# A graph layer with an eigenbasis on one core: another chain in each tridiagonal step, eight normalisation units a step, and VectorE statistics for eleven late batches

## The reference

```
h = relu(layernorm(x))                        # per batch and node, over 1024 features
Ln = D^-1/2 (D - A) D^-1/2                    # one 120x120 matrix, from adj
_, U = eigh(Ln)                               # its eigenvectors
agg = U h;  z = relu(agg @ W1 + b1) @ W2 + b2
f = softmax(theta(z) maxpool(phi(z)));  y = f maxpool(g(z))
w = batchnorm(wo(y)) + z
out = x + U w + w
```

## Time and profile before

| | us |
|---|---|
| median of 3 runs | 3356.74 (3353.61 to 3360.74) |
| the profiled execution | 3357.3 |
| its span, first to last instruction | 3355.5 |
| stage 1, to the last update of `QA` | 0 to 467.7 |
| stage 2, to GpSimd's first `fetch` | 467.7 to 669.4 |
| stage 3 | 669.4 to 3355.5 |

### The profile page before, as it was taken

The page is one execution under the profiler, slowest core; times in us unless marked ns, Lnnn a source line. Parts: engine busy times, 40 slices in busy tenths (PEclk is TensorE's granted clock), DMA queues, the critical chain, the costliest instruction groups (busy, mean ns, idle before and its releaser), DMA issues.

```text
span 3355.5 us, 65816 instructions
## 1 busy us (share of the span) xinstructions
PE 3177.8 (95%) x16040; PEld 2546.3 (76%) x16040; DVE 2290.7 (68%) x6009; ACT 2415.3 (72%) x4380; POOL 1950.8 (58%) x2073
## 2 busy tenths in 40 slices
PE   6888886699999999999999999999999999999997
PEld 5667776577777777777777777777777777777775
DVE  7877779766666666666666666666666666666664
ACT  6888998856666666667666667767666666767665
POOL 4333322146666666666666666666666666666665
PEclk9999999999999999999999999999999999999998
DMA  3333343312222222222222222222222222222222
GB/s 95 94 95 100 102 108 99 91 37 71 72 74 74 76 72 71 71 71 71 72 74 73 71 71 71 71 71 71 71 73 75 75 73 71 71 71 71 72 74 68
DMA packets 111575, 256.22 MB, mean 76 GB/s; under 512 B 47500, under 2 KB 49797, under 8 KB 111493
## 3 DMA queue, kind: packets, MB, share of 16 engines
q1 hardware_dynamic: 111493, 255.25, 27.8%
HBM read 190.69 MB, written 63.44 MB: 76 GB/s over the span
## 4 chain that ended last, share of the span: by engine, by line
PE 80%; DVE 10%; issue 3%; POOL 3%; ACT 3%; DVEq 0%; DMA 0%; POOLq 0%; ACTq 0%; SPq 0%
PE ps_M L793 8%; PE ps_M L795 8%; PE ps_M L794 8%; PE ps_S L870 7%; PE ps_E L793 7%; PE ps_O L793 7%; PE ps_E L794 7%; PE ps_O L795 7%; PE ps_O L794 7%; PE ps_E L795 7%; PE ps_M L854 3%; POOL sc L449 1%; DVE u L1024 1%; DVE rown L1022 1%; ACT junkx L536 1%
## 5 line engine op out<-in xcount | busy, mean ns | idle before, releaser
L502 POOL TENSOR_TENSOR p_lo<-p,p_hi 128x512 fp32r<-128x512 f32 x1024 | 1381.2, 1349 | 932.0 <-ACT p_hi L653 928.9
L648 ACT ACTIVATE p<-ps_E 128x512 f32<-128x512 f32 x1024 | 614.1, 600 | 331.8 <-PE ps_E L795 307.0
L1388 DVE TENSOR_REDUCE nmx<-ps_S 128x1 f32<-128x512 f32 x1024 | 658.6, 685 | 129.1 <-PE ps_S L870 126.3
L653 ACT ACTIVATE p_hi<-p 128x512 fp32r<-128x512 f32 x1024 | 647.5, 632 | 32.6
L793 PE MATMUL ps_E<-o_hi,Q_hi 123*128 123x512 f32 x1024 | 426.7, 417 | 0.0
L793 PE MATMUL ps_O<-p_hi,v_hi 128*121 128x512 f32 x1024 | 406.7, 397 | 3.9 <-POOL p_lo L502 3.8
L795 PE MATMUL ps_O<-p_lo,v_hi 128*121 128x512 f32 x1024 | 406.4, 397 | 0.0
L794 PE MATMUL ps_O<-p_hi,v_lo 128*121 128x512 f32 x1024 | 404.6, 395 | 0.0
L794 PE MATMUL ps_E<-o_hi,Q_lo 123*128 123x512 f32 x1024 | 404.5, 395 | 0.0
L795 PE MATMUL ps_E<-o_lo,Q_hi 123*128 123x512 f32 x1024 | 403.7, 394 | 0.0
L1368 DVE TENSOR_REDUCE gf<-ps_M 128x256 f32<-128x512 f32 x256 | 177.1, 692 | 261.8 <-PE ps_M L795 261.8
(11 more groups left out here) (363 smaller groups left out, 5939.8 us busy)
## 6 DMA issues: line engine op xcount, KB each, us to landing
rbc<-r_dram SPq DMA_DIRECT2D x128, 484.0 KB
xin<-in_x_dram SPq DMA_DIRECT2D x128, 480.0 KB, 4.2
xt<-in_x_dram SPq DMA_DIRECT2D x128, 480.0 KB, 4.9
out_dram<-y SPq DMA_DIRECT2D x128, 480.0 KB, 3.7
o_hi<-mrow SPq DMA_DIRECT2D x256, 2.0 KB
dcol<-y SPq DMA_DIRECT2D x128, 4.0 KB, 2.0
r_dram<-rcol SPq DMA_DIRECT2D x128, 4.0 KB, 1.4
W1s<-in_L_gnn_W_dram SPq DMA_DIRECT2D x1, 512.0 KB, 4.4
```

The lines of the kernel that those rows point to most:

```text
L502: pool.tensor_tensor(p_lo[:, c % 4, :], p[:, c % 4, :], p_hi[:, c % 4, :].bitcast(F32), ALU.subtract).then_inc(plo_sb, 1)
L648: act.activation(p[:, c % 4, :], ps_E[c % 2][:, :], ACT.Exp).then_inc(p_sb, 1)
L653: act.activation(p_hi[:, c % 4, :], p[:, c % 4, :], ACT.Copy).then_inc(phi_sb, 1)
L1388: dve.tensor_reduce(nmx[:, c:c + 1], ps_S[SBANK[c]][:, :], AX.X, ALU.max, negate=True).then_inc(max_sb, 1)
```

## The change

**The step.** The sign of the pivot moves from GpSimd to VectorE (`sign()`, four one-element instructions behind the update of `QA`, with two gates that hold factors -2 and -4). GpSimd keeps the power alone. VectorE applies root and sign in one instruction, the gated reciprocal goes straight into `cu`, the two one-element products L1013 and L1015 go, and the next `u` is formed from `cu`, a part row and one scalar (`PAIR`) that no longer reads `zs`. `QA` has two halves that are written in turn.

**The rate.** 8 units a step in place of 9, the last 3 of them behind the update: 920 units are placed at the end of stage 1.

**Statistics on VectorE.** For eleven batches (85, 88, ..., 115) ScalarE does neither mean nor squares. SyncE loads them into a part of `P1` not in use yet (two buffers `xdv`), VectorE forms mean and variance with two `BN_STATS` of 512 columns, a `BN_AGGR` and two scalings (`stats()`, in four parts), and ScalarE's relu of that batch waits for `stat_done`. `spare(us)` adds an amount to a counter at fixed places of stage 2 and puts in a part when the counter has reached 11.4 times the number of batches done; what is left is done behind `PS`. ScalarE's and SyncE's loops run to slot 84 and are written out from there.

**Places.** `GRID_AT` is 91, `WY_SLOT` 86, and the last products of the basis stand in TensorE's slots 127 to 129 (`basis`, `TAIL_AT`) instead of behind them. The transposes of two weights and the copy of them into `Cop` now stand at the grid product, and the row sums of `wn` behind the first copies of stage 2.

```diff
+            xdv = [P1[0:N, b * H:(b + 8) * H] for b in (B - 8, B - 16)]
...
+            def load_stat(n):
+                if n >= 2:
+                    sp.wait_ge(relu_done, BY_DVE[n - 2] + 1)
+                s = BY_DVE[n]
+                sp.dma_start(xdv[n % 2], x[s:s + 1, :, :].rearrange("a n d -> n (a d)")).then_inc(xd_in[n % 2], 16)
+            def load_late(a):
+                sp.wait_ge(sq_done, a - 1)
+                s = BY_ACT[a]
+                sp.dma_start(xin[:, a % 2, :], x[s:s + 1, :, :].rearrange("a n d -> n (a d)")).then_inc(x_in[a % 2], 16)
             load(0, 0)
             load(1, 1)
-            rounds(sp, 2, B, load)
+            rounds(sp, 2, UNROLL, load)
+            load_stat(0)
+            load_stat(1)
+            for a in range(UNROLL, len(BY_ACT)):
+                load_late(a)
+                for n in range(2, len(BY_DVE)):
+                    if BY_ACT[a - 2] == BY_DVE[n - 2] + 1:
+                        load_stat(n)
...
-                pool.wait_ge(u_ready, k + 1)
-                chain(pool.tensor_scalar(sc[:, SGN:SGN + 1], u[:, 1:2], 0.0, 2.0, ALU.is_ge, ALU.mult))
-                chain(pool.tensor_scalar(sc[:, SGN:SGN + 1], sc[:, SGN:SGN + 1], -1.0, None, ALU.add))
                 pool.wait_ge(s2_ready, k + 1)
-                chain(pool.tensor_tensor(sc[:, ROOT:ROOT + 1], sc[:, S2:S2 + 1], sc[:, 11:12], ALU.pow))
-                pool.tensor_tensor(sc[:, DU:DU + 1], sc[:, SGN:SGN + 1], sc[:, ROOT:ROOT + 1], ALU.mult).then_inc(du_ready, 1)
-                pool.tensor_scalar(sc[:, GATE:GATE + 1], sc[:, XN:XN + 1], TINY, -1.0, ALU.is_gt, ALU.mult).then_inc(gate_ready, 1)
...
+            def late_relu(s):
+                act.wait_ge(tr_done, s - 1)
+                a, n = by_act(s), by_dve(s)
+                if s in BY_DVE:
+                    act.wait_ge(stat_done, n + 1)
+                    act.activation(frelu[:, s % 2, :], xdv[n % 2], ACT.Relu, bias=lnd[:, n % 2, 0:1]).then_inc(relu_done, 1)
+                else:
+                    act.wait_ge(mean_done, a + 1)
+                    act.activation(frelu[:, s % 2, :], xin[:, a % 2, :], ACT.Relu, bias=lns[:, a % 2, 0:1]).then_inc(relu_done, 1)
...
+            def late_slot(k):
+                if k < B:
+                    late_relu(k)
+                    if k not in BY_DVE:
+                        late_sq(k)
+                if k - 2 < B:
+                    b_ft(k - 2, k % 2)
+                if k + 1 < B and k + 1 not in BY_DVE:
+                    late_sum(k + 1)
+                if k - 4 < B:
+                    b_p1(k - 4, k % 2)
...
                 if i == GRID_AT * UNITS:
+                    pe.wait_ge(wn_ready, 1)
+                    for j in range(1, 3):
+                        nc.tensor.transpose(ps_up[0:NA, H + j * H:2 * H + j * H], wn[:, j, :], ident[:, :])
                     pe.wait_ge(grid_below, 1)
                     mm(ps_up[0:N, 0:1], MJ[:, :], ones[:, 0:1], start=True, stop=True).then_inc(grid_count, 1)
                 norm_piece(i)
-
-            pe.wait_ge(p1_done, B)
-            for i in range(1, 3):
-                last = nc.tensor.transpose(ps_m[0][0:NA, (i - 1) * H:i * H], wn[:, i, :], ident[:, :])
-            last.then_inc(pe_out, 1)
-            pe.wait_ge(dve_out, 7)
-            nc.tensor.transpose(ps_up[0:N, 0:N], Z[:, :], ident[0:N, 0:N]).then_inc(pe_out, 1)
-            pe.wait_ge(wy_sb, WY_G + 3 + 21)
-            pe.wait_ge(dve_out, 8)
-            mm(ps_up[0:N, 0:N], QA[:, N:2 * N], VT[:, :], start=True, stop=True)
-            mm(ps_up[0:N, N:2 * N], VT[:, :], QA[:, N:2 * N], start=True, stop=True).then_inc(pe_out, 1)
-            pe.wait_ge(dve_out, 9)
-            mm(ps_up[:, 0:N], wos[:, :], Cop[0:N, 2 * H + 1:OPS], start=True, stop=True)
-            mm(ps_m[1][0:NA, 0:N], IA[:, :], Cop[0:N, 2 * H + 1:OPS], start=True, stop=True).then_inc(pe_out, 1)
+                if (i + 1) % UNITS == 0 and (i + 1) // UNITS - TAIL_AT in range(3):
+                    basis((i + 1) // UNITS - TAIL_AT)
...
+            def sign():
+                i_ge = did(TS(s_(SGN), u[:, 1:2], 0.0, 2.0, ALU.is_ge, ALU.mult))
+                did(TS(s_(GATE), s_(XN), TINY, -2.0, ALU.is_gt, ALU.mult))
+                did(TS(s_(GATE2), s_(XN), TINY, -4.0, ALU.is_gt, ALU.mult))
+                need(i_ge)
+                return did(TS(s_(SGN), s_(SGN), -1.0, None, ALU.add))
             dve.tensor_copy(u[:, 1:N], QA[0:1, 1:N]).then_inc(u_ready, 1)
             dve.wait_ge(u_ready, 1)
             norm(N)
-
-            def reflect(k):
+            signed = sign()
+            def reflect(k, signed):
                 L = N - k
                 par = k % 2
                 cu = cs[:, par, N:2 * N]
-                z_ = lambda i: zs[:, N + i:N + L]
-                dve.wait_ge(ry_ready, k + 1)
-                i_row = did(dve.tensor_copy(row1[:, k:N], ps_V[32:33, 0:L]))
-                dve.wait_ge(du_ready, k + 1)
-                i_u = did(T(u[:, 1:2], s_(DU), u[:, 1:2], ALU.add))
-                need(i_row)
-                i_z = did(STT(out=z_(0), in0=row1[:, k:N], scalar=s_(DU), in1=ps_V[0:1, 0:L], op0=ALU.mult, op1=ALU.add))
+                dve.wait_ge(root_ready, k + 1)
+                need(signed)
+                i_u = did(STT(out=u[:, 1:2], in0=s_(ROOT), scalar=s_(SGN), in1=u[:, 1:2], op0=ALU.mult, op1=ALU.add))
                 need(i_u)
                 i_uu = did(STT(out=srow[:, k:k + 1], in0=u[:, 1:2], scalar=u[:, 1:2], in1=s_(XN), op0=ALU.mult, op1=ALU.add))
-                need(i_z)
-                i_dot = did(STT(out=sqj[:, 0:L], in0=u[:, 0:L], scalar=1.0, in1=z_(0), op0=ALU.mult, op1=ALU.mult,
-                                accum_out=s_(AC)))
+                dve.wait_ge(ry_ready, k + 1)
+                i_row = did(TS(row1[:, k:N], ps_V[32:33, 0:L], s_(SGN), None, ALU.mult))
                 need(i_uu)
                 i_rec = did(dve.reciprocal(s_(REC), srow[:, k:k + 1]))
-                dve.wait_ge(gate_ready, k + 1)
+                need(i_row)
+                i_z = did(STT(out=zt[:, 0:L], in0=row1[:, k:N], scalar=s_(ROOT), in1=ps_V[0:1, 0:L], op0=ALU.mult, op1=ALU.add))
                 need(i_rec)
-                i_rg = did(T(s_(RG), s_(REC), s_(GATE), ALU.mult))
-                need(i_rg)
-                i_ac = did(T(s_(AC), s_(AC), s_(RG), ALU.mult))
-                i_cu = did(TS(cu[:, 0:L], u[:, 0:L], s_(RG), 2.0, ALU.mult, ALU.mult))
-                need(i_ac)
-                STT(out=z_(0), in0=u[:, 0:L], scalar=s_(AC), in1=z_(0), op0=ALU.mult, op1=ALU.add).then_inc(w_ready, 1)
+                i_cu = did(TS(cu[:, 0:L], u[:, 0:L], s_(REC), s_(GATE), ALU.mult, ALU.mult))
+                need(i_z)
+                i_dot = did(STT(out=sqj[:, 0:L], in0=u[:, 0:L], scalar=0.5, in1=zt[:, 0:L], op0=ALU.mult, op1=ALU.mult,
+                                accum_out=s_(AC)))
+                i_twice = did(TS(s_(PAIR), u[:, 1:2], s_(REC), s_(GATE2), ALU.mult, ALU.mult))
+                need(i_cu)
                 if k + 1 < STEPS:
-                    need(i_cu)
-                    dve.wait_ge(w_ready, k + 1)
-                    need(did(STT(out=rown[:, k + 2:N], in0=z_(2), scalar=cu[:, 1:2], in1=row1[:, k + 2:N],
-                                 op0=ALU.mult, op1=ALU.add)))
-                    STT(out=u[:, 1:L - 1], in0=cu[:, 2:L], scalar=zs[:, N + 1:N + 2], in1=rown[:, k + 2:N],
+                    i_part = did(STT(out=rown[:, 0:L - 2], in0=zt[:, 2:L], scalar=cu[:, 1:2], in1=ps_V[32:33, 2:L],
+                                     op0=ALU.mult, op1=ALU.add))
+                need(i_dot)
+                STT(out=zs[:, N:N + L], in0=cu[:, 0:L], scalar=s_(AC), in1=zt[:, 0:L], op0=ALU.mult, op1=ALU.add).then_inc(w_ready, 1)
+                now, then = par * N, (1 - par) * N
+                if k + 1 < STEPS:
+                    need(i_twice)
+                    i_pair = did(STT(out=s_(PAIR), in0=s_(PAIR), scalar=s_(AC), in1=zt[:, 1:2], op0=ALU.mult, op1=ALU.add))
+                    need(i_part)
+                    need(i_pair)
+                    STT(out=u[:, 1:L - 1], in0=cu[:, 2:L], scalar=s_(PAIR), in1=rown[:, 0:L - 2],
                         op0=ALU.mult, op1=ALU.add).then_inc(u_ready, 1)
                     dve.wait_ge(u_ready, k + 2)
+                    dve.wait_ge(w_ready, k + 1)
                     norm(L - 1)
                     dve.wait_ge(up_ready, k + 1)
-                    STT(out=XI[:, k + 2:k + 3], in0=ps_up[0:N, 2:3], scalar=QA[:, k + 1:k + 2],
+                    STT(out=XI[:, k + 2:k + 3], in0=ps_up[0:N, 2:3], scalar=QA[:, now + k + 1:now + k + 2],
                         in1=strict[:, k + 1:k + 2], op0=ALU.add, op1=ALU.mult).then_inc(xcol_ready, 1)
-                    dve.wait_ge(xcol_ready, k + 2)
                 dve.wait_ge(up_ready, k + 1)
-                T(QA[:, k:N], QA[:, k:N], ps_up[0:N, 1:L + 1], ALU.add).then_inc(a_ready, 1)
+                dve.wait_ge(a_ready, k + 1)
```

(38 more changed lines are left out.)

75 lines of the change are left out of this document (55 added, 20 removed).

## The result

The changed kernel takes **3435.08 us** (median of 5 runs, 3434.36 to 3461.47) against 3356.74 us: a ratio of 1.0253, 95% interval 1.0237 to 1.0268. That is slower, by 78 us, and far above the predicted 3363 (3346 to 3384). Both are used: the first for what it shows in excess, the second for the usual case.

A forecast was written before the change was run, and what follows sets the result against it. Stage 1 was taken as bound by a chain of small instructions through VectorE, GpSimd and TensorE, stage 2 by ScalarE with VectorE nearly level. Sum: 3357.3 - 55 + 61 = 3363 us, range 3346 to 3384.

The forecast's parts named there:

- Stage 1: The 117 steps of the chain: each 0.47 us shorter, 55 us gained, bounds 44 to 64 us.
- Stage 2: From the last update of `QA` to `fetch`: 262.9 us instead of 201.7, so 61 us more, bounds 50 to 75.
- The step, shift to `zs`: Stage 1 step, from the shift through row product, `cu` and part row to `zs`: 1.50 us, 0.12 longer than before.
- Power to shift: Stage 1 step, from GpSimd's power to VectorE's shift: 0.59 us instead of 0.85, as the product `DU` goes.
- the second rival: Stage 1: added one-element VectorE instructions delay the sign and row product; only 35 us gained, 3383 us; chance 0.16.
- `zs` to `u`, norm, sum, power behind the sum: The remaining links of a stage 1 step: 0.53, 0.33, 0.28 and 0.29 us.
- the first wait: Stage 2: VectorE stands still for the first statistics' data, 13.8 us (9 to 18).
- the eleventh statistics: Stage 2: the last batch's statistics, half of them behind `PS`, are done 199.0 us after the last update of `QA`.
- ScalarE's wait for them: Stage 2: ScalarE's relu of batch 115 waits some 20 us for VectorE's eleventh statistics.
- the last relu: Stage 2: ScalarE's relu of batch 127 comes 249.5 us after the last update of `QA`.
- The upper bound: Stage 2's highest cost: 75 us, from a first wait 4 us longer and 1.25 us more a batch, ten times.
- The lock of VectorE by GpSimd's power: Rival, stage 1: GpSimd's power holds VectorE's sign, shift 0.45 us later, 53 us in all, 3416 us; chance 0.04.

The follow-up runs named there:

- e13: e1 with both rows of TensorE's product at PSUM partition 0, as two one-row products: 3316.0 us, ratio 0.9878.
- e16: The changed kernel (eight units, statistics on VectorE) with both rows of TensorE's product at PSUM partition 0: 3386.1 us.
- e1: The changed kernel with nine units a step, grid and factors back at their earlier batches, and no statistics on VectorE: 3364.2 us, ratio 1.0015.
- e3: The changed kernel (new chain, eight units) with no batch's statistics on VectorE: 3403.4 us.
- e2: The kernel before (old chain, no statistics) with eight units a step, grid and factors at the changed kernel's batches: 3401.9 us.
- e10: The changed kernel with nine units, no statistics, old instructions from shift to column except one two-scalar instruction making the column from reciprocal and gate: 3340.3 us, ratio 0.9951.
- e11: The changed kernel run once more without any edit, giving its second profile: 3436.4 us.

## Why the prediction was wrong

The forecast was some 73 us too low. Stage 1 was to end 55 us sooner and ended 16 later: 71 us, of which about 60 are the chain's step and 11 the clock (the division is an estimate, worked out below). Stage 2 adds 2.

- **The step, shift to `zs`: the term that failed.** I had 1.50 us (at 85 columns), it took 2.00 (at 83). The row's scaling stood at 0.24 (I had 0.13), the product row 0.40 behind it (0.28), the part row 0.29 behind the factor (0.08), and the dot product 0.23 behind `cu` (0.17). The distances of 0.08 to 0.13 behind a one-element instruction were read in places where no PSUM read changes its start partition; the new chain changes it four times a step, the old one twice. e13 and e16 show it as the cause of 0.37 of the 0.52 us by which the step (4.06 for 3.54) was mis-sized. The rest is mostly in two places that stay in e13, each behind an instruction that takes two scalars from memory: the dot product 0.23 behind `cu`, and the part row 0.19 behind the factor. Why these are longer than I had them was not tested apart.
- **Power to shift**: 0.59 foretold, 0.66 measured (182.55 to 183.21). The power was done at 183.09, the copy behind the sign's instructions at 183.16, and the shift starts 0.05 behind the latter. That is the collision of the second rival, worth 0.07 us a step. With `XI` earlier (e13) the power ends last and the link takes 0.57.
- **`zs` to `u`, norm, sum, power behind the sum**: 0.53, 0.33, 0.28, 0.29 foretold; 0.51, 0.33, 0.27, 0.29 measured. Right.
- **The clock was no term at all.** I asked only whether TensorE would be late, and it would not. Its cost, from e1 with 34 us at half and e3 with 102: 7.6 us for 68, so some 10 us in the usual run (an estimate; e2 against the kernel before has 11.1 us for 62). The long stretch of the first profile, with steps of some 5.05 us, adds 28. Without the clock the new chain would end stage 1 some 5 us later than before, where I had -55 (an estimate from the 3.6 us that e1 loses in 107 full-clock steps, and 0.1 us in each of the other ten); of the 16.0 us that leaves 11 for the clock.
- **Stage 2 was right, to 2 us**: the first wait 14.8 (13.8), the eleventh statistics at +200.2 (+199.0), ScalarE's wait for them 18.9 (20), the last relu at +251.2 (+249.5), `fetch` +264.5 (+262.9). A `BN_STATS` lasts 0.69 us, the next instruction starts 0.60 us behind its start (I had 0.55). Not all of it was seen rightly. ScalarE waits for statistics five times, 33.1 us in all, not only at batch 115. And `fetch` waits for GpSimd's power of the last 64 batches, 10.53 us long, not for the basis; VectorE is done only 0.2 us before that power ends, so it is luck that the 13.4 us behind the last relu came out right. The upper bound adds up to 78, not 75.
- **The rivals.** The second, the step that wins less, had the direction but stopped at 35 us gained; no case had a step that gains nothing, which is why the range was too narrow. The lock of VectorE by GpSimd's power did not come: the sign's instructions run 0.06 us apart (182.79, 182.85) while it runs (182.55 to 183.09).

## What to carry to other kernels

When a chain of small VectorE instructions is laid out anew, note for each read of PSUM its start partition (here 0 or 32): where it differs from the last one's, count from the end of the instruction ahead, not 0.1 us. Before taking work from TensorE, look at its granted clock: here eight units in place of nine went with 65 to 191 us of stage 1 at half clock, and with none once the steps were 0.37 us shorter. And where an engine is to help another through two buffers that the other one frees, count its wait for the refill.

## What the runs showed of the hardware

- One start partition for two rows took 0.37 us off a step of 4.06 (e1 to e13, 83 columns). The changes to the instructions themselves took off 0.15 at most there (e10).
- In the first profile TensorE stayed at 1.2 GHz for 109 us in one piece, although it was busy 100.00 of 100 us in it. With two unneeded products a batch the clock was at half for 27 instead of 102 us. Why the first profile alone has the long stretch stays open; it was not tried apart.
- Behind a one-element instruction with two scalars from memory, one that does not need its result started 0.19 us later (159.12 to 159.31 in e13); behind a one-element instruction with constants it was 0.06 (182.79 to 182.85 in e11).
- The two `BN_STATS` of a batch last 0.69 us each for 120x512, and GpSimd's power 0.54 us for one element and 10.53 us for 120x64.
